# Read-out of a selective scan in eight half lumps, row loads in three pieces, four decay buffers

## The reference

```python
xn = (x - mu) / jnp.sqrt(var + 1e-05) * norm_w + norm_b
proj = xn @ x_proj_w.T
delta, B_ssm, C_ssm = jnp.split(proj, [R, R + N], axis=-1)
delta = jax.nn.softplus(delta @ dt_proj_w.T + dt_proj_b)
A = -jnp.exp(A_log)
C_used = C_ssm[:, jnp.arange(L) % CHUNK, :]          # CHUNK = 64

def step(h, inp):
    dt, b, xt, c = inp
    dA = jnp.exp(dt[:, :, None] * A)
    h = dA * h + dt[:, :, None] * b[:, None, :] * xt[:, :, None]
    y = jnp.einsum('bdn,bn->bd', h, c)
    return (h, y)
```

## Time and profile before

| | us |
|---|---|
| median of 3 runs (lowest, highest) | 1350.41 (1347.94, 1356.02) |
| the profiled execution | 1350.97 |
| its span, first to last instruction | 1349.1 |
| TensorE busy over the span | 1126.4 (83%) |
| VectorE busy | 846.0 (63%) |
| ScalarE busy | 500.5 (37%) |
| GpSimd busy | 306.3 (23%) |

### The profile page before, as it was taken

The page is one execution under the profiler, slowest core; times in us unless marked ns, Lnnn a source line. Parts: engine busy times, 40 slices in busy tenths (PEclk is TensorE's granted clock), DMA queues, the critical chain, the costliest instruction groups (busy, mean ns, idle before and its releaser), DMA issues.

```text
span 1349.1 us, 29055 instructions
## 1 busy us (share of the span) xinstructions
PE 1126.4 (83%) x11730; PEld 726.6 (54%) x11730; DVE 846.0 (63%) x1006; ACT 500.5 (37%) x1245; POOL 306.3 (23%) x930
## 2 busy tenths in 40 slices
PE   3647787889878887788886499999999597999998
PEld 2535444444444554454543288887777344465665
DVE  5859989899999999899995211112111477842211
ACT  3865554556555655555553011111111110121110
POOL 9641222222223222422232211111111200000000
PEclk8865868776888779876877599999999797999999
DMA  3897235433223222312214652222210400000000
GB/s 105 244 281 209 61 87 134 107 98 103 52 58 90 47 51 56 90 36 48 59 50 155 203 200 79 77 93 94 97 43 16 133 1 0 0 8 8 17 16 16
DMA packets 171685, 111.99 MB, mean 83 GB/s; under 512 B 93637, under 2 KB 162248, under 8 KB 169248
## 3 DMA queue, kind: packets, MB, share of 16 engines
q1 hardware_dynamic: 163120, 88.69, 23.7%
q0 software_dynamic: 8000, 20.87, 4.7%
q10 hardware_dynamic: 432, 0.59, 0.2%
HBM read 63.18 MB, written 45.90 MB: 81 GB/s over the span
## 4 chain that ended last, share of the span: by engine, by line
PE 52%; DVE 21%; issue 9%; SPq 7%; ACT 5%; DMA 3%; POOL 2%; DVEq 0%; POOLq 0%; ACTq 0%
DVE h L1151 13%; PE psum L1401 10%; PE psum L1413 10%; PE psum L1885 8%; PE psum L935 5%; PE psum L1896 4%; PE psum L921 4%; ACT decay L1036 3%; PE psum L902 3%; DVE den L1715 2%; PE psum L1841 2%; SPq L278 2%; DMA xdiag<-x_parts_d 1%; SPq L201 1%; SPq L199 1%
## 5 line engine op out<-in xcount | busy, mean ns | idle before, releaser
L1151 DVE TENSOR_TENSOR_SCAN h<-decay,psum 128x1024 f32<-128x1024 f32 x256 | 568.6, 2269 | 41.9 <-ACT psum L1046 34.5
L1036 ACT ACTIVATE decay<-psum 128x512 f32<-128x512 f32 x512 | 279.2, 600 | 211.1 <-PE psum L902 108.8
L921 PE MATMUL psum<-xdiag,bstat 96*128 96x64 bf16 x4096 | 199.9, 211 | 59.3 <-DVE h L1151 57.9
L921 PEld LDWEIGHTS psum<-xdiag,bstat 96*128 96x128 bf16 x4096 | 166.0, 109 | 86.7 <-DVE h L1151 77.3
L902 PEld LDWEIGHTS psum<-rows,shared 32*128 32x128 bf16 x4096 | 90.0, 104 | 221.2 <-issue 114.2
L935 PE MATMUL psum<-h,cstat 128*32 128x512 f32 x1024 | 187.2, 814 | 1.0 <-ACT y_raw L1088 1.0
L902 PE MATMUL psum<-rows,shared 32*128 32x64 bf16 x4096 | 123.9, 207 | 46.5 <-ACT decay L1036 38.0
L1401 PE MATMUL psum<-xdt,shared 128*128 128x320 f32 x512 | 141.4, 438 | 0.7 <-ACT xdt L1460 0.7
L1306 POOL TENSOR_TENSOR carry<-decay,h 128x16 f32<-128x16 f32 x240 | 57.9, 241 | 366.6 <-ACT decay L1036 366.4
L1413 PE MATMUL psum<-shared,hid 128*128 128x256 f32 x640 | 139.5, 379 | 0.6 <-ACT hid L1454 0.6
L1413 PEld LDWEIGHTS psum<-shared,hid 128*128 128x128 f32 x640 | 121.2, 190 | 17.0 <-issue 1.1
(11 more groups left out here) (192 smaller groups left out, 1044.1 us busy)
## 6 DMA issues: line engine op xcount, KB each, us to landing
shared<-in_w SPq DMA_DIRECT2D x16, 1024.0 KB, 4.8
xdiag<-x_parts_d SPq DMA_DIRECT2D x256, 48.0 KB
x_parts_d<-x_parts POOLq DMA_DIRECT2D x46, 256.0 KB, 8.0
parts_d<-dt_parts SPq DMA_DIRECT2D x24, 256.0 KB, 9.4
rows<-parts_d SPq DMA_DIRECT2D x128, 48.0 KB
disp_d<-zero SPq DMA_DIRECT2D x4, 1305.0 KB, 8.2
xd<-disp_d SPq DMA_DIRECT2D x8, 652.5 KB, 6.2
picked_d<-zero SPq DMA_DIRECT2D x4, 1024.0 KB, 5.7
```

The source lines that it names most:

```text
L921: ins = pe.q.matmul(to.rearrange("p d (s e) -> p s d e", e=2), bstat[0:ROWS, c % 2, b, :], xdiag[0:ROWS, c % 2, b, :, d, :], start=True, s ...
L1036: act.q.activation(decay[:, gi % NB, 8 * half:8 * half + 8, :], per_d(bank_a[half]), ACT.Exp).then_inc(sem("exp"), 1)
L1151: dve.q.tensor_tensor_scan(out=h[:, half_slot(c, half), ch:ch + G, :].rearrange("p d t -> p (d t)"), data0=decay[:, gi % NB, :, :].rearran ...
```

## The change

Four constants change, and with them the order of steps; the products are cut differently.

- The read-out takes eight half lumps: four of the first half of the channels, then four of the second, each with 256 columns and its own half of `bank_y`. They lie in seven of the eight groups: 0, 1, 2, (3 and 4), 5, 6, 7, and nothing in the eighth group. The last chunk's read-out, behind the scan, takes them in pairs.
- `y_sel` comes one group later.
- The 14 loads of a chunk come in three pieces (6, 4, 4 DMAs) at the groups 0, 1 and 2. The order within them stays.
- `NB` is 4: four buffers of `decay` and `carry`.

```diff
-LOADS = ((("dt", 0), ("dt", 1), ("dt", 2)), (("dt", 3), ("b", 0), ("b", 1)), (("x", 0), ("x", 1)), (("x", 2), ("x", 3)),
-         (("x", 4), ("x", 5)), (("x", 6), ("x", 7)))
+LOADS = ((("dt", 0), ("dt", 1), ("dt", 2), ("dt", 3), ("b", 0), ("b", 1)), (("x", 0), ("x", 1), ("x", 2), ("x", 3)),
+         (("x", 4), ("x", 5), ("x", 6), ("x", 7)))
...
-NB = 3
+NB = 4
...
-Y_STEPS = ((0,), (), (1,), (), (2,), (), (3,))
-Y_OUT, Y_PICK = 7, 8
+Y_STEPS = ((0,), (1,), (2,), (3, 4), (5,), (6,), (7,))
+Y_OUT, Y_PICK = 7, 9
...
-    for js in (js for js in Y_STEPS if js):
+    for js in ((0, 1), (2, 3), (4, 5), (6, 7)):
         yield ("y", CHUNKS - 1, js)
...
-                first, last = sorted((half_slot(c, 0), half_slot(c, 1)))
-                for j in js:
+                slots_of_h = sorted((half_slot(c, 0), half_slot(c, 1)))
+                for half, j in (divmod(n, 4) for n in js):
                     for q in range(4):
                         tok = 16 * q + 4 * j
-                        ins = pe.q.matmul(bank_y[32 * q:32 * q + 32, :].rearrange("p (s d e) -> p s d e", s=2, e=4),
-                                          s["cstat"][:, tok // 4, :], h[:, first:last + 1:last - first, :, tok:tok + 4],
+                        to = bank_y[32 * q:32 * q + 32, 256 * half:256 * half + 256].rearrange("p (d e) -> p d e", e=4)
+                        ins = pe.q.matmul(to, s["cstat"][:, tok // 4, :], h[:, slots_of_h[half], :, tok:tok + 4],
                                           start=j == 0, stop=j == 3)
-                if js[-1] == 3:
+                if js[-1] == 7:
                     ins.then_inc(sem("y"), 1)
```

## The result

The changed kernel takes 1361.08 us (median of 20 executions, 1357.04 to 1365.47); the kernel before, run beside it, 1355.67 (20 executions, 1347.94 to 1361.17). The ratio is 1.0049, with a 95% interval of 1.0033 to 1.0065: some 6.6 us slower, inside the 1% called "the same", where 14 us faster had been forecast, and outside the range. The profiled execution of after took 1365.47 us, at the slow end of its runs, that of before 1350.97, toward the fast end; so the two traces show more of the difference than the medians do. Its size is taken from the ratios, its place from the traces.

A forecast was written before the change was run, and what follows sets the result against it. It took VectorE's scans to bound the scan stage, with only 37.0 us of idle time to win, mostly from ScalarE's late hand-on. Gains of 5 + 6 + 3 = 14 us from 1350.4 gave 1336 us, range 1322 to 1356.

The forecast's parts named there:

- Edit 1: Read-out on TensorE in eight half lumps: shorter chain to the scan, forecast gain 5 us, bounds 18.7 gain to 19 loss.
- The 0.13 us that doesn't scale with the clock: Fixed part of a read-out burst on TensorE, the same at full and half clock, including any tile-shape switch.
- the further 0.4 us a chunk: Possible extra TensorE cost if each of three more bursts drained the engine again: 0.8 in place of 0.4 us a chunk.
- a third of 114 low groups: Scan groups at low clock taken to pay 0.33 us each, those beyond a spell's second: 38 groups, 12.5 us.
- the 18.7 us of the read-out: Part of VectorE's 37.0 us scan-stage idle time put down to what the read-out (L935) does to the chain.
- all 114, 38 us, a loss of 19: Worst bound for the half lumps: every low-clock group in the scan stage pays 0.33 us.
- one old-sized chain a chunk remains: Double burst of steps 3 and 4 on TensorE is as long as an old lump; no separate price given.
- Edit 2: Token loads in three pieces: late `xdiag` places in the scan go, gain 6 us, bounds 2 and 7.8.
- Edit 3: Fourth decay buffer: exponential starts 0.5 to 0.7 us earlier after disturbances, gain 3 us, bounds 0 and 5.
- clock worse, slower: Rival: half lumps leave TensorE's slow spells running on in the scan, 1369 us; sign 50.5 us of idle; chance 0.13.
- The first rival: Splitting read-out lumps gives 0 because TensorE bounds at half clock, other edits give 9: 1341 us; chance 0.30.
- Clock better: Rival: even TensorE work in the scan keeps the clock up, half lumps give 14 or more: 1327 us; chance 0.12.

The follow-up runs named there:

- e6_spread: The changed kernel with one half lump in each of the eight groups, no double burst, output copy a group later: 1393.61 us, ratio 1.0288.
- e8_warm_full: e4_nohalves with two added products, overwritten by the decays, in each group: 1345.76 us, ratio 0.9931 to the kernel before.
- e4_nohalves: The changed kernel with the old four lumps, keeping loads in three pieces, later `y_sel` and four buffers: 1341.75 us, ratio 0.9905 to the kernel before.
- e1_loads: The kernel before with only the loads in three pieces and `y_sel` a group later: 1345.34 us, ratio 0.9929.
- e9_fill: e4_nohalves with two added products, overwritten by the decays, in every second group, between the lumps: 1330.98 us, ratio 0.9834 to the kernel before.
- e12_spread_warm2: e6_spread with two added products, overwritten by the decays, in each group: 1345.75 us, ratio 0.9943 to the kernel before.
- e5_pairs: The changed kernel with its half lumps in pairs, in every second group, where the old lumps stood: 1345.71 us, ratio 0.9928 to the kernel before.
- e3_halves: The kernel before with only the read-out changed to eight half lumps over seven groups: 1371.71 us, ratio 1.0120.

## Why the prediction was wrong, point by point

- **What bounds the stage**: right for the whole of it. VectorE's busy time stayed within 4 us, but for e6_spread (594.37 us) and e8_warm_full (590.74), and the variants differ mainly by the idle time that ends with the hand-on. Only, at the low clock the pace is TensorE's, 2.5 us a group, and the forecast used this for the groups beyond the second alone.
- **Edit 1, durations**: right. Forecast 0.56 and 1.00 us a half lump, measured 0.57 and 1.01; a group at the low clock 2.50 forecast, 2.52 measured. The 0.13 us that doesn't scale with the clock held, and no more of it showed: single half lumps took what it gives, and the 16-record burst took 1.87 us like the old lump. So the further 0.4 us a chunk that the prediction weighed against more bursts did not show.
- **Edit 1, how many groups pay**: this step failed, and it carries most of the error. I let a third of 114 low groups cost 0.33 us, since the first two of each spell should be covered, so that the 18.7 us of the read-out would become 12.5. The two chunks from 228.60 us test this at the very clock that I had assumed, 0.77: VectorE idles 2.0 us in them, 31 us over 31 chunks. The low spell runs up to the double burst, and the slack that was to cover its first groups is used there: the 0.33 us are not forgiven but handed on. For the whole stage the same remainder is some 32 us, an estimate: 51.7 less 2.5 in the first chunk, 6.3 at the stumble, 4.1 before three table loads and 6.9 in two stretches of scatters. All 358/2.5 = 143 low groups at 0.33 us would be 47 us, so that is too much for the stage. Forecast for this edit: a gain of 5; measured: a loss of 19.5 (e4_nohalves against the changed kernel). That "all 114, 38 us, a loss of 19" stood as the bound and comes out so close is in part luck: its clock wasn't the one that came, and the old lumps too cost more at the low clock than the 18.7 us that it sets off. Their group is there (8 x 1.50 + 4 x 1.87) / 8 = 2.44 us in the mean, 0.27 over 2.17, and 286/2.44 = 117 groups make some 31 us. By this the half lumps win nothing at the low clock, 2.49 us a group in place of 2.44.
- **Edit 1, the clock**: taken as unchanged at 0.77, and this failed too: 0.72, and 56% of the stage (358 of 638.7) at the low clock in place of 46%. By the clock records of the two traces the low spells of the stage were 38 of 7.5 us in the mean before, and are 29 of 12.6 us: 51 groups beyond the second of their spell then, 91 now, where 38 had been reckoned with. The text had the two rows that speak to it, a fall after a thin stretch and a rise after a dense one, and used them only for rivals.
- **The double burst**: "one old-sized chain a chunk remains" was said, and given no price of its own. It is where 26.8 us of the stage's idle time stand. In every second chunk the transposes (L970) stand right behind it as well, and there the stall is 0.97 in place of 0.82 us; ScalarE then waits for them at L1097, 29.6 us in 15 pieces over the stage, which was 1.1 us before.
- **Edit 2**: right in mechanism and a little small: 6 forecast, 9.6 measured (e1_loads, 6.2 to 13.0 by the interval). The late `xdiag` places are gone but for the first, and none came back at `y_sb`: the only wait for it, 3.2 us, is as before and lies behind the scan. One thing was said too widely: the write and the loads of the earlier trace rows stand in one queue, SyncE's, so they show loads that land late behind a large write of the same queue, and nothing of several queues.
- **Edit 3**: 3 forecast; 3 on top of the loads, 1 alone, neither to be told from nothing. That the wait in the trace (101.7 us) isn't the gain was right.
- **The rivals**: "clock worse, slower" had the mechanism, at 0.13, and too high a price (1369), since it let every group be slow. In the profiled execution its mark was met: 51.7 us of idle time against 50.5, and 1.1% slower than before's; but with 91 groups beyond the second and not the 150 that it named, since it put all idle time on such groups. The first rival, that the lumps were not worth splitting because at the low clock TensorE itself is the bound, had the other half of the mechanism; it kept the clock as it was, and gave 1341. "Clock better" was wrong in its direction: here even work did not keep the clock up but let it fall. The Trainium skill (TensorE: Matmul & The Clock Gate, What's actually happening) says that throttled is the default and activity releases it; e9_fill and e12_spread_warm2 agree with it (0.80 to 0.92, 0.62 to 0.95 with added products), and e5_pairs, the changed kernel and e6_spread show that the same products release it less, the more evenly they lie.
- **The range** ended at 1356 and missed by 5 us. It leaned on the case that low groups come in short spells. The bound of a loss of 19 with the measured gains of the other edits, 9.6 + 3.3, would have given 1350.4 + 19 - 13 = 1356 at an unchanged clock; it stood at the very end of the range. The low end was added up wrongly: it took 2 us for the fourth buffer where 5 had been given as its bound, and would have been 1319. That the median of before rose from 1350.4 to 1355.7 us with more executions adds to the miss: by the ratio the changed kernel stands at 1350.4 x 1.0049 = 1357, still outside.

## What to carry to other kernels

If an engine's clock follows its work, splitting a lump of work and placing it evenly can cost more than the chain it shortens: read the granted clock of the stage before and after, and cost a group at either level against the pace of the engine that it feeds. Here the cure was the opposite of the change: keep the dense lumps and fill the thin groups between them with work that costs nothing, but only as much as fits beside that pace at full clock. A slack of two groups doesn't forgive a rate that is too slow where a long chain follows, it hands it to that chain; and a wait that goes (the exponential's for the scan) may only take another name.

## What the runs showed of the hardware that was not expected

- The clock of the scan stage is between 0.62 and 0.96 for the same computation, by the placement of TensorE's work and by one or two added products a group. Within the changed kernel's own 20 executions the time goes with it as well, on the whole: 1357.23 us at a mean clock of 0.841, 1365.47 at 0.826.
- In all thirteen kernels besides the one before, the profiled execution has one stumble of TensorE at the start of the seventeenth chunk: here in the changed kernel, the scans and TensorE's inputs.

```profile
410.21 0.32 PE L921 MATMUL psum<-xdiag,bstat 96*128 96x64 bf16 x3 [0.33 <-issue]
411.66 0.32 PE L921 MATMUL psum<-xdiag,bstat 96*128 96x64 bf16 x3 [1.12 <-issue]
411.78 2.29 DVE L1151 TENSOR_TENSOR_SCAN h<-decay,psum 128x1024 f32<-128x1024 f32 x1 [2.81 <-remote]
413.11 0.32 PE L921 MATMUL psum<-xdiag,bstat 96*128 96x64 bf16 x3 [1.14 <-issue]
```

TensorE gives out its sixteen products by threes with 1.1 us between them, in which it waits for nothing that the trace shows, and VectorE loses 2.81 + 1.07 + 2.42 = 6.3 us. In the other twelve the same scans lose 3.0 (e1_loads) to 6.4 us (e3_halves), in the profiled execution of before nothing. All three edits, alone or together, have it, so it is no mark of the read-out; whether other executions of the kernel before have it too isn't known, and neither is its cause.
